# A recurrent mixer kernel: products of two units in one run, a fourth decay buffer, selects on GpSimd

## The reference

```python
proj = hidden @ in_proj_w.T                     # gate, x, B, C (and dt)
xBC  = silu(causal_conv4(x_B_C) + bias)
dt_p = softplus(dt + dt_bias);  dA = exp(dt_p * -exp(A_log))
for t in range(512):                            # per head h, group g of h
    state = state * dA[t] + (dt_p[t] * x[t]) outer B[t]
    y[t]  = state @ C[t]
y   = y + x * D
yn  = y * rsqrt(mean(y*y over the group's 512 channels) + eps) * norm_w * silu(gate)
out = yn @ out_proj_w.T
```

## Time and profile before

| | |
|---|---|
| median of 3 runs | 3083.32 us (3082.72 to 3083.66) |
| profiled execution | 3077.91 us, its span 3076.4 us |
| TensorE busy | 3006.5 us, 98% of the span |
| VectorE | 2177.6 us, 71% |
| ScalarE | 1744.7 us, 57% |
| GpSimd | 644.8 us, 21% |
| granted TensorE clock | 0.996 of full speed on average |
| data moved by DMA | 444.86 MB, 145 GB/s on average |

### The profile page before, as it was taken

One profiled execution on the slowest core, in us unless ns is written; L12 is line 12 of the kernel. 1 busy time (PEld: TensorE's weight loads), 2 busy tenths in 40 slices (PEclk: granted clock), 3 DMA queues, 4 the chain that ended last, 5 costly groups with the idle time before them and its releaser, 6 DMA issues.

```text
span 3076.4 us, 45008 instructions
## 1 busy us (share of the span) xinstructions
PE 3006.5 (98%) x14304; PEld 2340.5 (76%) x14304; DVE 2177.6 (71%) x2660; ACT 1744.7 (57%) x3716; POOL 644.8 (21%) x447
## 2 busy tenths in 40 slices
PE   7999999999999998999999999999998999999998
PEld 6777777777777777777777777777776888887786
DVE  7667576676757687767676766767666878677877
ACT  3576575757566575576575757576675232234443
POOL 3322212121212234312222121222223000001112
PEclk9999999999999999999999999999999999999999
DMA  3434343333424353435243433334354444456665
GB/s 129 169 126 151 104 159 117 140 116 130 154 102 161 104 185 118 155 120 178 99 166 106 157 106 140 132 114 154 110 175 129 141 138 150 144 195 209 215 205 178
DMA packets 125528, 444.86 MB, mean 145 GB/s; under 512 B 17488, under 2 KB 21712, under 8 KB 109008
## 3 DMA queue, kind: packets, MB, share of 16 engines
q1 hardware_dynamic: 117552, 423.14, 41.0%
q0 software_dynamic: 4096, 14.68, 1.2%
q10 hardware_dynamic: 3744, 5.51, 0.5%
HBM read 397.86 MB, written 45.42 MB: 144 GB/s over the span
## 4 chain that ended last, share of the span: by engine, by line
PE 84%; DVE 6%; issue 6%; DMA 2%; ACT 2%; POOL 0%; SPq 0%; DVEq 0%; ACTq 0%; POOLq 0%
PE bank L1069 17%; PE bank L1071 17%; PE bank L1070 17%; PE bank L1107 8%; PE bank L1301 6%; PE bank L1302 6%; PE bank L1303 6%; PE bank L1081 2%; DVE acc L803 1%; PE bank L1093 1%; PE bank L1117 1%; DVE xbc L815 1%; DVE w_lo L785 1%; DMA acc<-in_w_out 1%; DMA units<-cum_scratch 1%
## 5 line engine op out<-in xcount | busy, mean ns | idle before, releaser
L1069 PE MATMUL bank<-x_hi,w_hi 128*128 128x512 f32 x2560 | 1023.9, 400 | 9.3 <-DVE acc L803 9.3
L1071 PE MATMUL bank<-x_hi,w_lo 128*128 128x512 f32 x2560 | 999.4, 390 | 0.0
L1070 PE MATMUL bank<-x_lo,w_hi 128*128 128x512 f32 x2560 | 997.3, 390 | 0.0
L803 DVE SCALAR_TENSOR_TENSOR acc<-bank,conv_w,acc 128x511 f32<-128x511 f32 (+2 forms) x576 | 430.7, 748 | 303.2 <-ACT acc L602 275.8
L1069 PEld LDWEIGHTS bank<-x_hi,w_hi 128*128 128x128 f32 x2560 | 480.6, 188 | 127.9 <-issue 23.1
L1071 PEld LDWEIGHTS bank<-x_hi,w_lo 128*128 128x128 f32 x2560 | 480.5, 188 | 104.2
L1070 PEld LDWEIGHTS bank<-x_lo,w_hi 128*128 128x128 f32 x2560 | 481.3, 188 | 93.6
L602 ACT ACTIVATE acc<-bank,tap_par 128x512 f32<-128x512 f32 x192 | 149.2, 777 | 579.7 <-PE bank L1071 434.1
L1301 PE MATMUL bank<-x_hi,w_hi 128*128 128x512 f32 x1024 | 402.5, 393 | 19.9 <-DVE x_lo L1293 15.6
L1302 PE MATMUL bank<-x_lo,w_hi 128*128 128x512 f32 x1024 | 400.4, 391 | 0.0
L1303 PE MATMUL bank<-x_hi,w_lo 128*128 128x512 f32 x1024 | 400.2, 391 | 0.0
(11 more groups left out here) (154 smaller groups left out, 3388.2 us busy)
## 6 DMA issues: line engine op xcount, KB each, us to landing
units<-cum_scratch SPq DMA_DIRECT2D x128, 1280.0 KB, 6.8
w_raw<-in_w_in SPq DMA_DIRECT2D x160, 512.0 KB, 3.7
w_raw<-y_scratch SPq DMA_DIRECT2D x128, 512.0 KB, 3.6
y_scratch<-gate SPq DMA_DIRECT2D x32, 1024.0 KB, 6.6
acc<-in_w_out SPq DMA_DIRECT2D x128, 256.0 KB, 3.8
xbc<-in_x SPq DMA_DIRECT2D x16, 512.0 KB, 6.3
units<-in_x SPq DMA_DIRECT2D x16, 512.0 KB, 3.7
rstd_b<-rc_scratch SPq DMA_DIRECT2D x32, 256.0 KB, 4.1
```

The source lines that it names most:

```text
L803: dve.scalar_tensor_tensor(acc[:, s % 2, back:], bank_proj[s % 2][:, 0:SEQ - back], mix.conv_w[:, at, m, 3 - back:4 - back], acc[:, s % 2, ...
L1069: pe.matmul(out, w_hi[m % 2][:, k, :], hi, start=(k == 0), stop=False)
L1070: pe.matmul(out, w_hi[m % 2][:, k, :], lo, start=False, stop=False)
L1071: mm = pe.matmul(out, w_lo[m % 2][:, k, :], hi, start=False, stop=(k == KT - 1))
```

## The change

- **Plans.** `mult` stands in pairs: both sequences of a channel tile follow each other in one slot, in LATER at slots 11, 15, 19 and 23. The transposes stand in pairs too; exp and attn slots are lists of their own. The normalisation of both sequences starts in one slot (26 in LATER, `norm_after`), where it was 25 and 23 before.
- **Banks and buffers.** A second transposing bank (bank 7, which also holds a part of the scores), a fourth decay buffer (RING is 4). To make room, `w_raw`, `th`, `rstd_b` have one buffer where they had two, and the mask is 256 wide. With one `rstd_b`, SP issues the load for the second sequence after GpSimd has scaled the first.
- **Decays by whole rows.** GpSimd writes a large number over the entries before the diagonal (`hide`, four selects for a unit, L482 after the change); then ScalarE makes the decays of a head with four Exp of 512, 384, 256 and 128 columns, which read a bias and a factor of −1 (L657 after the change). The scores are copied instead of being multiplied by the mask.
- **The rest.** `tanh` and `gate_in` wait until the one `th` has been read. The weights of the small projection at the second half wait for unit 6 (of 8) where they waited for unit 5. The first two tiles of the output projection are loaded at slots 15 and 16, and its input lies in `xbc`.

The diff, cut to its core:

```diff
+NEVER = 32768.0
...
-RING = 3
+RING = 4
...
-        self.w_raw = sb("w_raw", [P, 2, KT, P])
+        self.w_raw = sb("w_raw", [P, KT, P])
...
-        self.acc, self.th = sb("acc", [P, 2, SEQ]), sb("th", [P, 2, SEQ])
+        self.acc, self.th = sb("acc", [P, 2, SEQ]), sb("th", [P, SEQ])
...
-    def __init__(self, cb, load, mult, gate_from, exp=None):
+    def __init__(self, cb, load, exp, attn, turn, mult, gate_from, norm_after):
         self.cb, self.bc = cb, [s + 1 for s in cb]
-        self.load, self.mult = load, mult
-        self.exp = exp or [s - 3 + h for s in mult for h in range(2)]
-        self.turn = [s - 2 for s in mult]
-        self.attn = [s - 1 for s in mult]
+        self.load, self.exp, self.attn, self.turn, self.mult = load, exp, attn, turn, mult
+        self.hide = exp[0::2]
         self.square = [s + 1 for s in mult]
         self.gate = [max(s + 1, gate_from + 1 + u) for u, s in enumerate(mult)]
-        self.norm = [s + 2 for s in mult[-SEQS:]]
-        self.var = [s + 3 for s in mult[-SEQS:]]
-        self.rc = [s + 4 for s in mult[-SEQS:]]
-        self.rb = [s + 5 for s in mult[-SEQS:]]
-        self.scale = [s + 6 for s in mult[-SEQS:]]
-        self.store = [s + 7 for s in mult[-SEQS:]]
+        self.norm = [s + norm_after for s in mult[-SEQS:]]
+        self.var = [s + 1 for s in self.norm]
+        self.rc = [s + 2 for s in self.norm]
+        self.rb = [s + 3 for s in self.norm]
+        self.scale = [s + 4 for s in self.norm]
+        self.store = [s + 5 for s in self.norm]
...
-FIRST = Plan(cb=[9, 11], load=[9, 10, 12, 14, 15, 17, 19, 20], mult=[13, 14, 16, 18, 19, 21, 23, 24],
-             gate_from=CONV_SLOTS)
-LATER = Plan(cb=[4, 6], load=[4, 5, 7, 10, 12, 14, 16, 18], mult=[9, 11, 13, 15, 17, 19, 21, 23],
-             gate_from=CONV_SLOTS)
-LAST = Plan(cb=[4, 6], load=[4, 5, 7, 10, 12, 14, 15, 17], mult=[9, 11, 13, 14, 16, 18, 20, 21],
-            gate_from=CONV_SLOTS, exp=[6, 7, 8, 9, 10, 11, 11, 12, 13, 14, 15, 16, 17, 18, 18, 19])
+FIRST = Plan(cb=[9, 11], load=[9, 10, 12, 13, 16, 17, 19, 20],
+             exp=[10, 11, 12, 13, 13, 14, 15, 16, 17, 17, 18, 19, 20, 20, 21, 22],
+             attn=[12, 14, 16, 17, 19, 20, 22, 23], turn=[13, 13, 15, 15, 18, 18, 21, 21],
+             mult=[15, 15, 18, 18, 21, 21, 24, 24], gate_from=CONV_SLOTS, norm_after=2)
+LATER = Plan(cb=[4, 6], load=[5, 6, 9, 10, 13, 14, 17, 18],
+             exp=[6, 7, 8, 9, 10, 11, 12, 13, 14, 15, 16, 17, 18, 19, 20, 21],
+             attn=[8, 10, 12, 14, 16, 18, 20, 22], turn=[8, 8, 11, 11, 15, 15, 19, 19],
+             mult=[11, 11, 15, 15, 19, 19, 23, 23], gate_from=CONV_SLOTS, norm_after=3)
+LAST = Plan(cb=[4, 6], load=[5, 6, 8, 9, 12, 13, 15, 16],
+            exp=[6, 7, 8, 9, 9, 10, 11, 12, 13, 13, 14, 15, 16, 16, 17, 18],
+            attn=[8, 10, 11, 13, 15, 16, 18, 19], turn=[8, 8, 11, 11, 14, 14, 17, 17],
+            mult=[11, 11, 14, 14, 17, 17, 20, 20], gate_from=CONV_SLOTS, norm_after=2)
...
+OUTPUT_LOADS = [SLOTS - 5, SLOTS - 4]
...
-    bank_tr = core.bank[2]
+    bank_tr = [core.bank[2], core.bank[7]]
...
-    rstd_b = sb("rstd_b", [P, SEQS, SEQ])
+    rstd_b = sb("rstd_b", [P, SEQ])
...
-            need(sp, w_split, n - 1)
-            sp.dma_start(w_raw[:, m % 2, :, :], w_tiles[TILES * at + ORDER[m]]).then_inc(w_loaded[m % 2], 16)
+            need(sp, w_split, n)
+            sp.dma_start(w_raw[:, :, :], w_tiles[TILES * at + ORDER[m]]).then_inc(w_loaded, 16)
...
-                sp.dma_start(rstd_b[:, q, :], d["rc"][q].partition_broadcast(P)).then_inc(rstd_loaded[q], 16)
+                need(sp, scaled, SEQS * g + q)
+                sp.dma_start(rstd_b[:, :], d["rc"][q].partition_broadcast(P)).then_inc(rstd_loaded[q], 16)
...
-            need(sp, multiplied, UNITS * (half * GROUPS - 1) + UNITS - 2)
+            need(sp, multiplied, UNITS * (half * GROUPS - 1) + UNITS - 1)
...
-                    ahead = s // 2 + 3
+                    ahead = s // 2 + 2
                     if ahead < TILES:
                         load_w(g, at, ahead)
                     elif not ends_all(half, plan):
                         load_w(g + 1, after(at, plan), ahead - TILES)
-                    elif ahead < TILES + 2:
-                        sp.wait_ge(w_split, TILES * g + ahead - 1)
-                        sp.wait_ge(silu_done, CONV_SLOTS * (g + 1))
-                        output.load(sp, 0, 0, ahead - TILES)
+                if ends_all(half, plan) and s in OUTPUT_LOADS:
+                    sp.wait_ge(cb_done, SEQS * (g + 1))
+                    sp.wait_ge(silu_done, CONV_SLOTS * (g + 1))
+                    output.load(sp, 0, 0, OUTPUT_LOADS.index(s))
...
+        def hide(g, u):
+            r = u % RING
+            pool.wait_ge(cum_loaded[r], 16 * (RING_USES[r] * g + u // RING + 1))
+            pool.nop(nofuse=True)
+            for k in range(CHUNKS):
+                near = attn[r][:, :, OFFSET[k]:OFFSET[k] + P]
+                op = pool.affine_select(out=near, in_=near, compare_op=ALU.is_ge, fill=NEVER, base=0,
+                                        pattern=[[0, 2], [1, P]], channel_multiplier=-1)
+            op.then_inc(hidden, 1)
...
+            for u in due(plan.hide, s):
+                hide(g, u)
...
+            if s:
+                act.wait_ge(silu_done, CONV_SLOTS * g + s)
+            else:
+                need(act, gate_done, GATE_SLOTS * g)
+            act.activation(th[:, :], acc[:, s % 2, :], ACT.Tanh).then_inc(tanh_done, 1)
...
-                act.wait_ge(silu_done, CONV_SLOTS * g + s - 1)
                 need(act, stored[q], 16 * g)
+            if v:
+                act.wait_ge(gate_done, GATE_SLOTS * g + v)
             else:
-                act.wait_ge(gate_done, GATE_SLOTS * g + v - 1)
-            act.activation(th[:, s % 2, :], bank_proj[s % 2][:, :], ACT.Tanh, scale=0.5).then_inc(tanh_done, 1)
+                act.wait_ge(silu_done, CONV_SLOTS * (g + 1))
...
-            if h == 0:
-                act.wait_ge(cum_loaded[u % RING], 16 * (RING_USES[u % RING] * g + u // RING + 1))
+            act.wait_ge(hidden, UNITS * g + u + 1)
             for k in range(CHUNKS):
-                part = tile[:, OFFSET[k]:OFFSET[k] + P]
-                op = act.activation(part, part, ACT.Relu, bias=mix.cum[:, CHUNKS * q + k, head], scale=-1.0)
-            op.then_inc(fall_done, 1)
-            for k in range(CHUNKS - 1):
-                part = tile[:, OFFSET[k] + P:OFFSET[k] + WIDTH[k]]
-                act.activation(part, part, ACT.Exp, bias=mix.dec[:, CHUNKS * q + k, head])
-            act.wait_ge(fall_done, 2 * UNITS * g + 2 * u + h + 1)
-            near = tile[:, 0:2 * WIDTH[0]].rearrange("p (a b) -> p a b", b=WIDTH[0])[:, :, 0:P]
-            act.activation(near, near, ACT.Exp, scale=-1.0)
-            step = WIDTH[2]
-            near = tile[:, OFFSET[2] - P:OFFSET[2] - P + 2 * step].rearrange("p (a b) -> p a b", b=step)[:, :, P:step]
-            op = act.activation(near, near, ACT.Exp, scale=-1.0)
+                part = tile[:, OFFSET[k]:OFFSET[k] + WIDTH[k]]
+                op = act.activation(part, part, ACT.Exp, bias=mix.falls[:, CHUNKS * q + k, head], scale=-1.0)
             if h == 1:
...
-                op = dve.tensor_tensor(bc[:, q, OFFSET[k]:OFFSET[k] + WIDTH[k]], cb_out[k],
-                                       core.mask[:, 0:WIDTH[k]], ALU.mult)
+                op = dve.tensor_copy(bc[:, q, OFFSET[k]:OFFSET[k] + WIDTH[k]], cb_out[k])
...
-            need(pe, dtx_done, UNITS * g + u)
+            need(pe, dtx_done, UNITS * g + u - 1)
+            if u == 1:
+                pe.wait_ge(bc_done, SEQS * (g + 1))
             if first and u == 0:
                 pe.wait_ge(early_of[half].mix_copied, NT)
             for k in range(CHUNKS):
-                mm = pe.transpose(bank_tr[:, k * P:(k + 1) * P], xbc[:, c, toks(q, k)], core.ident[:, :])
+                mm = pe.transpose(bank_tr[u % 2][:, k * P:(k + 1) * P], xbc[:, c, toks(q, k)], core.ident[:, :])
...
+        pe.wait_ge(dtx_done, UNITS * HALVES * GROUPS)
         pe.wait_ge(bc_done, SEQS * HALVES * GROUPS)
         pe.wait_ge(gate_taken, GATE_SLOTS * HALVES * GROUPS)
         first_products((3, 4, 7, 0, 1))
-        drain(piece, HALVES - 1, SLOTS + 1, SLOTS + 3)
+        drain(piece, HALVES - 1, SLOTS + 1, LAST.norm[0])
         pe.wait_ge(y_done, UNITS * HALVES * GROUPS)
         first_products((5, 6))
-        drain(piece, HALVES - 1, SLOTS + 3)
+        drain(piece, HALVES - 1, LAST.norm[0])
...
-        self.y_raw = mix.w_raw[:, :, :, :].rearrange("p a k c -> p a (k c)")
+        self.y_raw = mix.xbc[:, XT:, :]
```

86 lines of the change are left out of this document (43 added, 43 removed).

## The result

The changed kernel takes 3175.64 us (median of 4 runs, 3172.73 to 3181.01) against 3083.02 before: ratio 1.0302, 95% interval 1.0285 to 1.0320. It is slower by 93 us, where 3095 was predicted and 3122 was the upper end. The profiled execution was the longest of the four: 3181.01, span 3179.5, so 103.1 us over the span of before.

The account below looks back on a forecast made before the run. TensorE, busy 139.33 of 140.07 us, bounds it. Middle groups +15.6, FIRST −2.8, LAST −1.5, boundary +4, tail −3 make +12.3: profiled 3077.9 becomes 3090.2, or 3095 as median of runs; range 3046 to 3122.

Parts of the forecast that it names:

- Edits at zero, ScalarE: Four Exp a head in place of nine activations: some −330 us of ScalarE work, no gain in itself.
- Pairing: Products in pairs pay 0.35 us for the half-array form once for two units: −1.4 us per middle group.
- no saving by pairs: Rival: the 0.35 us is paid per unit or bank, so 22 us is lost: 3118; chance 0.06.
- The new wait: Middle groups, slot 14: bank free at X+42.6 (X: end of slot 7's projection), about 3.2 us late, 3.4 with restart.
- The old wait in slot 11: Middle groups' 0.65 us convolution wait, about 0.9 with restart: 0.2 taken to remain, −0.7 per group.
- The clock: Clock near full throughout the kernel before, so no term for it in the sum.
- FIRST and LAST at zero: First and last groups of a half: new wait 0 for both, but +2 us for half 0's LAST.
- Selects: GpSimd's selects: 0.38 us each, 1.5 a unit, 12 a group, on an engine busy 30 of 140 us.
- The boundary: At the second half, the small weights' load waits for one more unit: +4 us, bounds −2 and +8.
- The tail's −3: First wait of the output projection: −3 us, last product a slot earlier and tiles loaded earlier; bounds −6 and +6.
- One `w_raw` at zero: Single weight buffer costs nothing: a load of some 4 us has two slots, 10.9 us, cover 7 us.
- Reloading: Rival: GpSimd alternating selects with products reloads code, about 6 us in 12 groups: 3167; chance 0.02.

Follow-up runs that it names:

- run 4: Changed kernel with two rstd_b buffers and unit 2's load and selects a slot earlier in middle groups: 3113.60 us; the same without pairs there: 3112.13.
- run 6: Changed kernel without the selects (no masking, Tanh for Exp): 3098.86 us, 1.0041; with two rstd_b buffers besides: 3132.85 us, 1.0165.
- run 8: Changed kernel with single products everywhere, two rstd_b buffers, early selects: 3107.94 us; pairs in middle groups only: 3126.78; singles, small weights early: 3096.19.
- run 1: Changed kernel, in middle groups unit 2's load in slot 8 and selects in slot 9, ahead of both scales: 3135.61 us, 1.0169.
- run 7: Kernel before, with only the middle groups' normalisation of both sequences started in slot 26, both scales in slot 10: 3128.93 us, 1.0147.
- runs 4 and 9: 9: changed kernel with singles, small weights early, unpaired middle plan; unit 2's load in slot 7, selects in 8: 3132.87 us; each a slot later: 3078.61.
- run 2: Changed kernel with two rstd_b buffers, so the second load doesn't wait for the first scale: 3160.93 us, 1.0247.

## Why the prediction was wrong

The direction and the central chain were right, the size was not: 93 us against 12. By the profiled executions (103 against 12) some 32 us of the difference stand in the ten steady groups, some 55 in the other six, where nearly nothing had been forecast, and 4 in the start and the output part.

- *Edits at zero, ScalarE.* Near: 1446.8 us against 1420, and no gain to be seen from it.
- *Pairing.* The price was right. Transposes and product of a pair take 5.53 us of TensorE, where 5.5 was predicted (194.60 to 200.36, less one projection step of 0.23):

```profile
194.60 1.03 PE L1109 MATMUL bank<-ident,xbc 128*128 128x128 f32 x8
195.57 4.53 PE L1123 MATMUL bank<-units,dtx 128*64 128x512 f32 x32
200.36 0.39 PE L1083 MATMUL bank<-x_lo,w_hi 128*128 128x512 f32 x1
```

  But it was counted as time, and pairs also bring their own 1.1 us of waits a group (run 4). Rival "no saving by pairs" holds for the time and not for the mechanism.
- *The new wait.* Predicted 3.2 us ahead of slot 14, behind ScalarE's gate operation; measured 3.13, in the place and by the chain named (scale, rb, scale, selects, Exp; ScalarE standing 9.03 against 9). Slot 13 was missed: 1.2 us on the convolution of slot 11, which hangs on the same late tap, so the chain was 4.4 late in all. The old wait in slot 11 went, and 0.30 us in slot 10 came, near the 0.2 that was left for it. (In the prediction the bank is free at X+42.6 and wanted at X+39.2, which are 3.4 apart and not 3.2; the slip is small.)
- *The clock.* This term was missing. The sum went by the clock's 1.00 of before. The 3.1 us wait is followed in eight of the ten steady groups by a stretch at a granted 0.50. Between first and last projection such stretches cost 30 of the 103 us.
- *FIRST and LAST at zero.* **This is the step that failed.** The prediction looked only at the place of unit 2's selects against the scales: it put the cost of the selects in the last groups at nothing, and took groups 1 and 9, where the first group's late pairs fall, for middle groups like the others (+1.3 us each). They grew by 13.9 and 15.0, group 7 by 20, group 15 by 5. Without the selects groups 0, 1, 7, 8 and 9 fall by 32 us together (run 6). There the selects stand on GpSimd behind paired sums and gate products that VectorE's operations stretch. The timeline at the start of group 1 in the changed kernel shows it:

```profile
191.83 6.10 POOL L463 TENSOR_TENSOR gate<-gate,units 128x512 f32<-128x512 f32 x2
192.88 3.91 DVE L853 TENSOR_TENSOR units<-units,bc 128x2560 f32<-128x2560 f32 x1
197.89 1.48 POOL L482 TENSOR_SCALAR_AFFINE_SELECT units<-units 128x256 f32<-128x256 f32 x4
199.40 3.74 ACT L657 ACTIVATE units<-units,falls 128x512 f32<-128x512 f32 x8 [7.37 <-POOL units L482]
215.51 0.47 PE L1082 MATMUL bank<-x_hi,w_hi 128*128 128x512 f32 x1 [3.53 <-DVE acc L816]
```

  ScalarE stands 7.37 us for the selects, the tap and the convolution behind it come late, and TensorE waits 3.53.

- *Selects.* 0.37 us each alone, as estimated (0.38), but 1.15 beside the product with the scores, 0.63 on average. The sentence that the port rule "asks for no term" was an error too: the trace agrees with the rule of the Trainium skill, "SBUF — State Buffer", section "SBUF: two separate sides", in the other direction as well (VectorE's operation holds GpSimd's), and 4.59 against 1.48 us is that term.
- *The boundary.* The small weights cost 6.8 (run 8, with single products), between the 4 and its bound of 8; but group 7 grew by 20: pairs and late selects came on top (without the selects it is 12 less), and the clock was 0.95. The tail's −3 didn't come: the output part took 1.8 us more.
- *One `w_raw` at zero.* Right in the middle groups of the changed kernel, wrong there as soon as the larger wait is gone (run 1): the cover of 7 us is used up by SP's in-order wait for a scale. Wrong in groups 0 and 8, where ScalarE stood for this load (3.42 us at 68.36, 2.56 at 82.42; run 8 shows the second).
- *Reloading.* Selects and products follow each other on GpSimd without a gap (1788.30 + 4.55, then 1792.80): no such price.

How far is it explained? Taking the selects out gives 77 of the 93 us (run 6); leaving them in and mending their order and the second rstd_b load gives 62 (run 4). These two overlap and are not a sum. Of the rest, single products take away what groups 1 and 9 had over, and the early small weights what the front had (run 8). What groups 0 and 8 keep is open; one `w_raw` is a cause that the trace suggests and no run tried.

## What to carry to other kernels

When work is moved off an engine with slack onto GpSimd, ask first what waits in line behind it there and which of VectorE's operations will run beside it. In these runs a GpSimd operation and one of VectorE with two operands in SBUF hardly overlapped: together they took about the sum of their lengths. VectorE's convolution steps, which read a bank and one operand in SBUF, kept their length. Price a new wait of TensorE of about 3 us with the half clock behind it, and check every group kind (first, middle, last), since the same change cost 4.4 us in a middle group and 20 in the group ahead of the front. Two long GpSimd operations back to back cost 4.3 us a group where a silu and the low split fell beside them (run 7), and nothing where they began behind the low split (runs 4 and 9).

## What the runs showed of the hardware

- GpSimd and VectorE's operations with two operands in SBUF block each other both ways: silu 0.68 to 4.60 us (run 7), low split 1.21 to 5.63 (run 6, two buffers), four selects 1.48 to 4.59, two gate products 2.49 to 6.10.
- VectorE's 576 convolution steps, with one operand in a bank, took 0.73 to 0.75 us in the changed kernel, beside GpSimd's work or not.
- Two waits of TensorE of 3.13 and 3.14 us, at the same place of two groups, were followed by a granted clock of 0.50 for 5.8 us in the one and 1.00 in the other. What decides between them was not found. In run 2 a wait of 2.65 us (until 710.62) was followed by 0.50 from 711.6 to 715.0.
